# Another order of the instructions in the attention phase of a post-norm transformer block on one core

## The reference, cut to what matters

```python
q1, q2, k1, k2 = heads(x, Wq1), heads(x, Wq2), heads(x, Wk1), heads(x, Wk2)   # 16 channels each
v = heads(x, Wv)                                                               # 32 channels
att1 = softmax(where(mask, q1 @ k1.T * scale, -inf))
att2 = softmax(where(mask, q2 @ k2.T * scale, -inf))
y = (att1 - lam * att2) @ v
yn = groupnorm(y over time and groups) * gn_w + gn_b; yn = yn * gamma * (1 - LAMBDA_INIT)
x = layernorm(x + yn @ Wc.T)
```

## Time and profile before

| what | us |
|---|---|
| median of 3 runs | 6410.7 (6407.92 to 6411.48) |
| the profiled execution, own time | 6412.27 |
| its span in the profile | 6410.2 |
| TensorE busy | 5903.5 (92%) |
| VectorE busy | 4155.1 (65%) |
| ScalarE busy | 3490.4 (54%) |
| GpSimd busy | 883.9 (14%) |

### The profile page before, as it was taken

The page is one execution under the profiler, slowest core; times in us unless marked ns, Lnnn a source line. Parts: engine busy times, 40 slices in busy tenths (PEclk is TensorE's granted clock), DMA queues, the critical chain, the costliest instruction groups (busy, mean ns, idle before and its releaser), DMA issues.

```text
span 6410.2 us, 146596 instructions
## 1 busy us (share of the span) xinstructions
PE 5903.5 (92%) x58112; PEld 2663.7 (42%) x58112; DVE 4155.1 (65%) x10780; ACT 3490.4 (54%) x6980; POOL 883.9 (14%) x1873
## 2 busy tenths in 40 slices
PE   8999999999999999986999999999999999999985
PEld 3443434343433434332444444444444444444432
DVE  5777777777777777764565655656565565655533
ACT  4666666666666666563545454554545545454532
POOL 2222222222222222220000000000000000000000
PEclk9999999999999999997999999999999999999997
DMA  3223233333323233321000000000000000000004
GB/s 68 49 50 65 51 61 52 62 52 55 56 49 65 49 63 53 56 40 61 11 11 11 14 7 14 11 11 14 19 18 7 14 11 11 14 7 14 11 22 143
DMA packets 137129, 232.17 MB, mean 36 GB/s; under 512 B 40476, under 2 KB 40604, under 8 KB 135680
## 3 DMA queue, kind: packets, MB, share of 16 engines
q1 hardware_dynamic: 136448, 222.83, 16.8%
HBM read 53.86 MB, written 33.55 MB: 14 GB/s over the span
## 4 chain that ended last, share of the span: by engine, by line
PE 69%; DVE 11%; ACT 10%; issue 8%; DMA 2%; SPq 0%; POOL 0%; POOLq 0%; DVEq 0%; ACTq 0%
PE ps L548 20%; PE ps L677 14%; PE ps L770 9%; PE ps L885 6%; PE ps L910 4%; PE ps L821 4%; PE ps L860 4%; PE ps L841 2%; ACT pt L1073 2%; DVE mc L1374 2%; PE ps L829 2%; ACT sm L1187 2%; ACT gates L1230 2%; PE ps L803 1%; DVE rr L1535 1%
## 5 line engine op out<-in xcount | busy, mean ns | idle before, releaser
L1073 ACT ACTIVATE pt<-ps 128x1024 f32<-128x1024 f32 (+7 forms) x2048 | 1235.7, 652 | 747.2 <-PE ps L548 525.1
L1370 DVE CUSTOM_DVE_ANT_0 junk<-ps,causal 128x128 bf16<-128x128 f32 (+3 forms) x2048 | 988.4, 487 | 439.8 <-PE ps L548 422.7
L548 PE MATMUL ps<-kt,qt 96*32 96x512 bf16 (+3 forms) x12288 | 1066.4, 332 | 100.1 <-DVE mc L1374 55.7
L677 PE MATMUL ps<-pt,ones 128*32 128x512 f32 (+3 forms) x6144 | 1150.9, 489 | 0.0
L677 PE MATMUL ps<-pt,vs 128*32 128x512 f32 (+3 forms) x3072 | 1147.1, 488 | 0.0
L677 PE MATMUL ps<-pt,va 128*32 128x512 f32 (+3 forms) x3072 | 1143.8, 487 | 0.5 <-POOL pt L1740 0.4
L548 PE MATMUL ps<-qt,kt 98*32 98x512 bf16 (+3 forms) x12288 | 827.8, 328 | 42.0 <-ACT pt L1073 32.7
L1374 DVE TENSOR_REDUCE mc<-ps 128x1 f32<-128x512 f32 x1024 | 704.2, 688 | 99.7 <-PE ps L548 77.1
L770 PE MATMUL ps<-wqkv,xs 128*128 128x512 f32 x1536 | 739.1, 614 | 13.8 <-DMA wqkv<-in_wqkv 13.8
L1740 POOL TENSOR_SCALAR_AFFINE_SELECT pt<-pt 128x256 f32<-128x256 f32 x1024 | 456.2, 446 | 2137.3 <-ACT pt L1073 2137.3
L1187 ACT ACTIVATE sm<-sm,mxw 128x256 f32<-128x256 f32 (+1 forms) x1024 | 496.7, 486 | 428.2 <-DVE mxw L1543 427.8
(11 more groups left out here) (147 smaller groups left out, 8584.5 us busy)
## 6 DMA issues: line engine op xcount, KB each, us to landing
qt<-part SPq DMA_DIRECT2D x768, 64.0 KB, 2.4
kt<-part SPq DMA_DIRECT2D x768, 64.0 KB, 2.5
ya<-wy SPq DMA_DIRECT2D x128, 128.0 KB, 2.3
yb<-wy SPq DMA_DIRECT2D x128, 128.0 KB, 2.3
xs<-between_phases SPq DMA_DIRECT2D x32, 512.0 KB, 3.8
between_phases<-xo SPq DMA_DIRECT2D x32, 512.0 KB, 2.8
xt<-in_x SPq DMA_DIRECT2D x16, 512.0 KB, 6.3
between_phases<-z SPq DMA_DIRECT2D x16, 512.0 KB, 2.8
```

What stands on the lines that cost most here:

```text
L548: mmi = pe.matmul(ps[32 * q:32 * q + 32, bank, lo:hi], weights[:, 32 * q:32 * q + 32], moving, start=start, stop=stop)
L677: mmi = pe.matmul(ps[32 * q:32 * q + 32, 4 + half, lo - half * 512:hi - half * 512], w, probs(kb)[:, i, lo - first(kb):hi - first(kb)], st ...
L1073: act.activation(probs(kb)[:, i, kb * P - first(kb):1024 - first(kb)], ps[:, 2 * i:2 * i + 2, :].rearrange("p a q -> p (a q)")[:, kb * P:1 ...
L1370: ins = dve.tensor_tensor_reduce(out=junk[:, bank - 6, 0:w], in0=ps[:, bank, 0:w], in1=causal[:, 512 - w:512], scale=1.0, scalar=NEG, op0= ...
```

## The change

The diff, cut (the TensorE part writes out the order above):

```diff
-T_AT = 6
+T_AT = 4
...
-                next_scores(2, (1, 1))
-                weigh(1, (0, 1))
...
+                weigh(0, 0, 1)
+                next_scores(2, 0, 1)
+                weigh(0, 1, 1)
...
+                next_scores(4, 0, 0)
+                weigh(3, 0, 1)
+                weigh(3, 1, 1)
+                next_scores(4, 1, 1)
+                unit(0, 0, 0)
+                unit(0, 1, 1)
...
@@ ScalarE
-                    if kb == 6:
-                        copy_out(g, 0)
-                        extra_second(g, 1)
+                exps(g, 6)
+                copy_out(g, 0)
+                exps(g, 7)
+                extra_second(g, 1)
...
@@ VectorE
                         if k == T_AT:
                             copy_maxima(g + 1, slot + k)
-                        if k == T_AT + 1 and g:
+                        if k == 8 and g:
                             normalise(g - 1)
                         piece(g + 2, k, slot + slot_of(k))
-                        if k == 9 and h % 4 == 1 and g > 4:
+                        if k == 11 and h % 4 == 1 and g > 4:
                             over_time(g // 4 - 1)
-                        if k == 13:
+                        if k == 15:
                             extra(g, 0)
                         if k == 17:
                             extra(g, 1)
                         if h % 4 == 0 and g:
-                            if k == 15:
+                            if k == 13:
                                 sum_group(g // 4 - 1)
-                            if 20 <= k <= 21:
-                                half_statistics(g // 4 - 1, k - 20)
-                            if k == 23:
+                            if k == 14:
+                                half_statistics(g // 4 - 1, 0)
+                            if k == 16:
+                                half_statistics(g // 4 - 1, 1)
+                            if k == 18:
                                 statistics(g // 4 - 1)
-                        if h == 4 and b and k == 21:
+                        if h == 4 and b and k == 17:
                             divide(b - 1, 0)
                         if h == 5 and b and k == 3:
                             divide(b - 1, 1)
```

More of the change, by code:

```diff
@@ L711, in pieces, with next_scores @@
                     count += n
-                def next_scores(kb, beside):
+                def next_scores(kb, i, then):
                     follow = (g, kb) if kb < 8 else (g + 1, 0)
[L715 to L731, removed]
+                    if follow[0] < ALL:
+                        scores(follow[0], follow[1], i)
+                    pieces(then)
+                def weigh(kb, n, then):
+                    values(g, kb, n)
+                    pieces(then)
+                def unit(e, part_of, then):
+                    extra(g, e, part_of)
+                    pieces(then)
@@ L732, in _ @@
+                next_scores(1, 0, 1)
+                next_scores(1, 1, 1)
+                weigh(0, 0, 1)
+                next_scores(2, 0, 1)
+                weigh(0, 1, 1)
                 if g == ALL - 2:
                     max_transpose(g + 1, slot)
-                next_scores(2, (1, 1))
-                weigh(1, (0, 1))
[L736 to L749, removed]
+                next_scores(2, 1, 1)
+                weigh(1, 0, 2)
+                weigh(1, 1, 0)
+                next_scores(3, 0, 1)
+                next_scores(3, 1, 1)
+                weigh(2, 0, 0)
@@ new lines, in _ @@
+                weigh(2, 1, 1)
+                next_scores(4, 0, 0)
[4 more added lines that the diff above has]
+                unit(0, 1, 1)
+                next_scores(5, 0, 1)
+                next_scores(5, 1, 0)
+                unit(1, 0, 1)
+                unit(1, 1, 0)
+                next_scores(6, 0, 0)
+                next_scores(6, 1, 1)
+                weigh(4, 0, 1)
+                weigh(5, 0, 0)
@@ L751, in _ @@
+                next_scores(7, 0, 0)
+                next_scores(7, 1, 2)
+                next_scores(8, 0, 1)
+                next_scores(8, 1, 1)
+                weigh(6, 0, 1)
+                weigh(7, 0, 0)
             b = nb - 1
@@ L1130, in _ @@
                 b, h = divmod(g, HEADS)
[L1131 to L1143, removed]
-                    if kb == 6:
-                        copy_out(g, 0)
-                        extra_second(g, 1)
+                exps(g, 0)
+                if g:
+                    copy_out(g - 1, 1)
+                exps(g, 1)
+                if g:
+                    invert(g - 1)
+                    if h % 4 == 1 and g > 4:
+                        over_time(g // 4 - 1)
+                exps(g, 2)
+                exps(g, 3)
+                exps(g, 4)
+                extra_first(g, 0)
+                exps(g, 5)
+                extra_second(g, 0)
+                extra_first(g, 1)
+                exps(g, 6)
+                copy_out(g, 0)
+                exps(g, 7)
+                extra_second(g, 1)
             copy_out(ALL - 1, 1)
```

## The result

The changed kernel takes 6225.1 us (median of 4 runs, 6224.4 to 6226.5) against 6409.3 us; the ratio is 0.9713, 95% interval 0.9696 to 0.9730. The forecast was 6227 us in a range of 6150 to 6320. The profiled execution took 6224.4 us, its span is 6222.3.

The account below looks back on a forecast made before the run. No engine is full; TensorE, in fixed order, meets things not ready. Walked heads sum to 331.4 against 354.8 us a batch, 1.46 a head, x 126 = 184 us, giving a median of 6227 us, range 6150 to 6320.

Parts of the forecast that it names:

- The stake: TensorE's array waits 2.95 us a head for things not ready: at most 372 us to win over 126 heads.
- walk: Ordinary head followed instruction by instruction in the new order, with prices from the trace: 20.0 us instead of 21.42.
- ScalarE's step: End of head: second bf16 part moves behind E(7,1), so E(7,0) starts 0.52 us earlier; S(8,0) waits 0.3, not 0.66.
- rival B: Only ScalarE's step pays, other waits return behind other pieces: 0.52 us in 9 of 16 heads, 37 us, 6374; chance 0.08.
- `normalise`: On VectorE, moved from ahead of p7 to ahead of p8; before, p8, p9 and p10 paid 0.7 us for it.
- The charge for meeting the mask: Block 2's mask starts just before `normalise`: 0.2 to 0.3 us charged to `normalise`, a 0.3 wait to p10.
- `over_time`: At h%4 == 1 it adds 0.5 us on ScalarE ahead of E(2), putting block 2's mask behind `normalise`: 20.5 us.
- rival A: `normalise` starts before block 2's mask in all heads; V(2,0) loses 0.9, p10 regains 0.3: 76 us, 6303; chance 0.15.
- The norm's heads: Heads h = 3 at 20.6 and h = 4 at 21.1 us, waiting for centring and squares; h = 5 at 21.2.
- rival C: Slower: V(3,0), ahead of S(4,1), waits for block 3's mask in every head: +30 us, 6441; chance 0.07.

## Why the prediction was right

**The stake and the method.** The forecast counted waits of the array by start-to-start times, not by the busy row, and moved each instruction by hand. It gave 331.4 us a batch; the trace has 331.5, and 331.4 to 332.3 in the other full batches. The mechanism is the one foretold: fewer waits, the same work. The exact match is partly luck, from errors that cancel. These are the waits in us of head 87, each the time from start to start less what the columns between take:

| wait at | before | walk | after |
|---|---|---|---|
| S(1,1), V(0,0) | 0.27, 0.08 | 0.2, 0.1 | 0.10, 0.08 |
| p5, p7 (before), p4 (after) | 0.13, 0.06 | 0.07 | 0.09 |
| p8, p9, p10 | 0.30, 0.20, 0.21 | 0, 0, 0.3 | 0, 0, 0.14 |
| S(7,1), p21 | 0.21, 0.17 | 0.15, 0 | 0.10, 0 |
| S(8,0) | 0.66 | 0.3 | 0.36 |
| sum | 2.29 | 1.1 | 0.87 |

The difference, 1.42 us, is the whole gain of the head. Another 0.32 us of the head, in both kernels, are some 0.004 at each of about 75 changes from one group of matmuls to the next. They are no waits, the new order left them as they were, and the walk had no term for them.

The step from a head to the program also held two errors. The heads without extra units, in the first and the last batch, fell from 19.61 to 17.41 us, by 2.2 and not by 1.46, which is most of why the last transpose is 191 us earlier and not 184 (2 of the 7 us lie ahead of the first transpose). Of that, 3 us go in the rest of the program, and 4 are the difference between the two profiled executions and their medians. And the low end of the range does not follow from its own words: 0.25 and 0.6 us a head less make 6120, not 6150. Nothing hung on it.

**ScalarE's step**, 0.52 us: shown by adding it (23 us) and removing it (29 us). Its size in an ordinary head was right, its place in the sum too; what I had not said is that alone it would be lost at h%4 == 0, which makes rival B's 37 us too much.

**`normalise`**: that the old order gave no gain by its move, and the new one needs it ahead of p8, are both shown (0 and 79 us, for 0 and 74 expected). The charge for meeting the mask was mis-sized: 0.2 to 0.3 forecast, 0.04 measured, and p10 waits 0.14 instead of 0.3. The ordinary head came out at 20.00 all the same because the 0.32 us of small steps took the place of what was charged too much. Wrong as well was that p8, p9 and p10 had all paid for `normalise` before: the 0.3 at p8 was not its doing, as the run of `normalise` alone shows.

**`over_time`**: its effect on the mask of block 2 was named and mis-sized. I forecast 20.5 us for h = 9 and 23.9 for h = 1; they took 20.86 and 24.25, since V(2,0) waits the full 0.9. That is rival A's mechanism, in 24 heads and not in all, and dearer than A's 0.6 us a head: only the 0.14 at p10 comes back, not 0.3, so 0.8 is lost. What decided was what the prediction said would decide, the order of two starts 0.2 us apart.

**The norm's heads** were too dear: in the batch shown h = 3, 4 and 5 took 20.42, 20.51 and 20.78 us instead of 20.6, 21.1 and 21.2. These 1.2 us cancel the 1.0 by which the three heads with `over_time` were too cheap.

**V(3) ahead of S(4,1)**, rival C: refuted. V(3,0) starts without a wait (0.22 us after S(4,0) starts, which takes 0.21), and to put the scores first again changes nothing. The time that I expected to be just enough is enough; the exchange is simply not a part of the gain.

**Rival B**, that the waits come back elsewhere, is true of single moves on VectorE in the old order (`normalise` alone: nothing won), and false of the whole. What carries the whole is the pair of TensorE's and VectorE's new orders, 160 us together: inside it the place of `normalise` is worth 79 us and that of the first residue 48. I did not run TensorE's new order alone, nor the new places of the statistics, so how the 160 us divide is not shown.

The Trainium skill's rule on VectorE and GpSimd (SBUF — State Buffer, "Who interferes with whom"), that the order of issue decides which of the two blocks, is borne out in both directions of order: in head 89, with `normalise` first, the mask takes 1.3 us instead of 0.41, and in head 87, with the mask first, `normalise` takes 1.26 instead of 1.22. The last section has the measure of the loss.

## What to carry to other kernels

Where no engine is full, count the gaps of the busiest one from start to start, and ask of each which instruction ahead of the awaited one could stand elsewhere; a move on the waiting side and a move on the awaited side often pay only together. Put instructions whose input is late (a residue behind a projection) where the engine has nothing else queued behind them. Let two instructions that shut each other out start in the order in which the short one goes first: here half a microsecond of small work on a third engine turned that order round and cost 0.9 us.

## What was not expected of the hardware

The charge for the meeting of `normalise` and the mask took the second instruction to lose all the time for which the first one still runs. It loses about 0.15 us less, in either order. The mask, started 0.12 us after `normalise` in the run with `normalise` before p7, took 1.37 us instead of 0.41: it lost 0.96, while `normalise` still ran for 1.10. In every meeting of that order, in this run, in the kernel before, in the changed one and in the run of `normalise` alone, the mask ends 0.27 us after `normalise`, wherever inside it started.

The other order does the same. `normalise`, started when the mask still ran for 0.19, lost 0.04. VectorE's small operations with two SBUF inputs show it for longer overlaps. In the kernel before:

```profile
2031.46 0.17 DVE L1379 TENSOR_TENSOR mm<-mc 128x16 f32<-128x16 f32 x1
2031.87 0.41 POOL L1740 TENSOR_SCALAR_AFFINE_SELECT pt<-pt 128x256 f32<-128x256 f32 x1 [0.90 <-ACT pt L1073]
2031.88 0.42 DVE L1383 TENSOR_TENSOR nm<-mm,nm 128x16 bf16<-128x16 f32 x1
```

and in the changed one:

```profile
1902.35 0.41 POOL L1756 TENSOR_SCALAR_AFFINE_SELECT pt<-pt 128x256 f32<-128x256 f32 x1 [0.39 <-ACT pt L1084]
1902.54 0.24 DVE L1393 TENSOR_TENSOR mm<-mc 128x16 f32<-128x16 f32 x1
```

Such an operation takes 0.17 to 0.18 us without a mask. Started 0.01 after one, it lost 0.25 of the 0.40 left, and started 0.19 after, 0.07 of 0.22. So the exclusion holds in full both ways, and `normalise` lost only 0.04 because it came when the mask was nearly done. Started together with the mask but behind it, it would have lost some 0.26, an estimate from 0.41 less 0.15. To have the short instruction first is cheap because it is short: the second one can lose no more than the length of the first, 0.41 us here against 1.22.
